# Keys and queries for pairs of tiles, a kept row made on ScalarE, and new orders, in a fused decoder layer

## The reference

```python
def _L0_attn_ref(...):                      # x = x + this(layernorm(x))
    t = tokens * rsqrt(mean(tokens * tokens) + eps) * rms_w
    gates = sigmoid(t @ w_gates)            # one per head
    q, k, v = t @ wq, t @ wk, t @ wv        # 8 heads of 64
    attn = softmax(where(causal_mask, -max, q @ k.T * scale))
    return sum over heads of ((attn @ v) * gates) @ wo

def _L0_xattn_ref(...):                     # x = x + this(layernorm(x), ctx, ctx)
    u = q @ k.T * scale / sqrt(8)           # 16 heads of 8, no projections
    logits = where(mask, -inf, tanh(u) * exp(log_C))
    return softmax(logits) @ v @ W_out.T

def _L0_ffn_ref(x, ...):                    # x = x + this(layernorm(x))
    xn = layernorm(x) * g + b
    probs = softmax(clip(xn @ router_w.T))
    topk_p, topk_i = top_k(probs, 2)        # 2 of 8 experts
    for eid in range(8):
        xe = xn * dense_gate[:, eid]
        hidden = silu(gate) * up            # of xe @ gate_up_w[eid].T
        out = out + hidden @ down_w[eid].T
    return x + out
```

## Time and profile before

| | us |
|---|---|
| median of 3 runs | 259.38 |
| lowest and highest run | 257.85, 260.14 |
| the profiled execution's own time | 259.18 |
| its span in the profile | 257.4 |
| busy in it: PE | 224.5 (87%) |
| busy in it: DVE | 197.1 (77%) |
| busy in it: ACT | 144.0 (56%) |
| busy in it: POOL | 128.2 (50%) |
| mean granted clock of PE | 0.958 of full speed |

### The profile page before, as it was taken

One profiled execution on the slowest core, in us unless ns is written; L12 is line 12 of the kernel. 1 busy time (PEld: TensorE's weight loads), 2 busy tenths in 40 slices (PEclk: granted clock), 3 DMA queues, 4 the chain that ended last, 5 costly groups with the idle time before them and its releaser, 6 DMA issues. The chain is left out here.

```text
span 257.4 us, 9580 instructions
## 1 busy us (share of the span) xinstructions
PE 224.5 (87%) x3360; PEld 184.5 (72%) x3360; DVE 197.1 (77%) x874; ACT 144.0 (56%) x333; POOL 128.2 (50%) x184
## 2 busy tenths in 40 slices
PE   8888999999999999999999988857987999989800
PEld 2666877886886887877777755436977899989700
DVE  2558687898898889989888897968995777766343
ACT  2455776885776776777667656424332355545400
POOL 1122321413546746646556356636777776656630
PEclk9999999999999999999999999975999999999965
DMA  7995999300000000000000001065774888888376
GB/s 221 254 374 215 401 410 406 135 3 4 3 12 26 14 13 24 14 13 25 13 14 21 16 0 35 24 174 179 218 216 116 268 275 230 268 239 250 94 237 190
DMA packets 24526, 36.31 MB, mean 141 GB/s; under 512 B 3726, under 2 KB 14225, under 8 KB 24224
## 3 DMA queue, kind: packets, MB, share of 16 engines
q1 hardware_dynamic: 20272, 29.98, 36.3%
q0 software_dynamic: 2272, 4.27, 4.7%
q10 hardware_dynamic: 1936, 1.46, 1.9%
HBM read 21.26 MB, written 14.89 MB: 140 GB/s over the span
## 5 line engine op out<-in xcount | busy, mean ns | idle before, releaser
L1959 POOL TENSOR_TENSOR rstd<-var,cst 128x1 f32<-128x1 f32 (+1 forms) x32 | 25.8, 807 | 73.8 <-DVE var L1300 48.7
L2058 POOL DMA_INDIRECT results<-y_sb,meta x39 | 38.3, 981 | 16.9 <-DVE xw_sb L1707 9.1
L505 PE MATMUL six<-gT_sb,gu_sb 128*128 128x128 f32 x312 | 43.3, 288 | 0.6 <-issue 0.6
L505 PEld LDWEIGHTS six<-gT_sb,gu_sb 128*128 128x128 f32 x312 | 39.4, 201 | 1.0 <-issue 0.8
L2016 POOL DMA_INDIRECT slots<-pay,slot_i x32 | 33.2, 1038 | 11.9 <-issue 7.0
L1093 ACT ACTIVATE jsilu<-six 128x256 f32<-128x256 f32 x39 | 14.9, 383 | 21.8 <-PE six L505 21.8
L1690 DVE TENSOR_TENSOR hidT<-jsilu,six 128x256 f32<-128x256 f32 x39 | 16.2, 416 | 10.7 <-PE six L505 10.7
L505 PE MATMUL six<-downT_sb,hidT 128*128 x156 | 23.6, 278 | 0.7 <-DVE hidT L1690 0.7
L1029 ACT ACTIVATE etanh<-six,xscale 128x1024 f32<-128x1024 f32 x16 | 17.8, 1113 | 7.1 <-PE six L505 7.1
L505 PEld LDWEIGHTS six<-downT_sb,hidT 128*128 128x128 f32 x156 | 20.3, 192 | 1.2 <-issue 1.1
L505 PEld LDWEIGHTS six<-wo_sb,oT_sb 128*128 128x128 f32 x128 | 15.5, 191 | 6.4 <-issue 6.4
(11 more groups left out here) (159 smaller groups left out, 537.8 us busy)
## 6 DMA issues: line engine op xcount, KB each, us to landing
gu_sb<-in_guT SPq DMA_DIRECT2D x39, 256.0 KB, 3.7
slots<-empty_sb SPq DMA_DIRECT2D x16, 528.0 KB, 5.9
g_sb<-slots SPq DMA_DIRECT2D x39, 66.0 KB, 3.4
ctxT_all<-in_ctxT SPq DMA_DIRECT2D x1, 1024.0 KB, 8.7
downT_sb<-in_downT SPq DMA_DIRECT2D x1, 1024.0 KB, 9.8
y_all<-results SPq DMA_DIRECT2D x4, 256.0 KB, 3.6
x_all<-in_x SPq DMA_DIRECT2D x2, 320.0 KB, 3.7
results<-y_sb,meta POOLq DMA_INDIRECT x39
```

What stands on the lines that cost most here:

```text
L505: return pe.matmul(o, lhsT=l, rhs=r, start=start, stop=stop, **kw)
L1959: nc.gpsimd.tensor_tensor(dst, src, half[:, 0:dst.shape[1]], ALU.pow).then_inc(semaphore, 1)
L2058: nc.gpsimd.indirect_dma_start(results, bass.IndirectOffsetOnAxis(meta[j % (2 * RING)][:, 0:1].bitcast(I32), 0), y_sb[k][:, :], None, boun ...
```

## The change

**Keys and queries.** `tT_sb` now holds two tiles side by side. `project_k` and `project_q` are replaced by `project_lo(n)` and `project_hi(n)`: with n even they make the keys of tiles n and n + 1, with n odd the queries of tiles n - 1 and n; lo makes the first four of the eight heads and hi the others, two products of 256 columns each. One n is done per step, two steps ahead of the tile, and `turn_t` and `normalize` run three ahead, so that the loop begins at i = -3. The number and the size of ACT's copies are as before.

**The kept row.** `norm_xhat` and POOL's `carry` go. POOL's `line` makes two numbers per row, 1 + rstd and -mean * rstd, and ACT's `carry` writes x2 * (1 + rstd) - mean * rstd in one Identity operation.

**Orders.** PE, DVE, ACT and POOL have new orders in `step` and in the drain.

```diff
-        tT_sb = several("tT_sb", [P, P])
-        qT_sb = several("qT_sb", [P, NJ, P])
-        k_sb = several("k_sb", [P, NJ, P])
+        tT_sb = several("tT_sb", [P, 2, P])
+        q_sb = several("q_sb", [P, NJ, 2, P], n=2)
+        k_sb = several("k_sb", [P, NJ, 2, P], n=2)
...
+            def project_pair(n, bank, j0):
+                w = wq_sb if n % 2 else wk_sb
+                both = tT_sb[n // 2 % BUFS].rearrange("p u t -> p (u t)")
+                for m in range(2):
+                    ins = mm(bank[:, m * 2 * P:(m + 1) * 2 * P], w[:, (j0 + m) * P:(j0 + m + 1) * P], both)
+                return ins
...
+            def project_lo(n):
+                after(pe, tT_ready, n | 1)
+                after(pe, lo_ready, n - 1)
+                after(pe, oT_ready, n - 3)
+                project_pair(n, ko_bank, 0).then_inc(lo_done, 1)
...
+            def project_hi(n):
+                after(pe, hi_ready, n - 1)
+                after(pe, pT_ready, n - 3)
+                after(pe, tanh_ready, n - 4)
+                project_pair(n, qp_bank, NJ // 2).then_inc(hi_done, 1)
...
             def scores(t):
-                after(pe, qT_ready, t)
-                after(pe, k_ready, t)
+                after(pe, lo_ready, query_fill(t))
+                after(pe, hi_ready, query_fill(t))
...
             def turn_p(t):
                 after(pe, weighed, t)
-                if has(t + 1, 0):
-                    after(pe, qT_ready, t + 1)
+                if has(t + 2, 0):
+                    after(pe, hi_ready, t + 2)
...
             def step(i):                                    (PE)
+                if has(i, 1):
+                    attend(i - 1)
                 if has(i, 0) and i > 0:
                     gates(i)
-                if has(i, 1):
-                    attend(i - 1)
-                if has(i, -1):
-                    turn_t(i + 1)
                 if has(i, 3):
                     cross_project(i - 3)
+                if has(i, -3) and i != -1:
+                    turn_t(i + 3)
...
-                    project_k(i + 1)
-                    project_q(i + 1)
+                if has(i, -2):
+                    project_lo(i + 2)
+                    project_hi(i + 2)
...
             def step(i):                                    (ACT)
                 if has(i, 4):
                     turn_xn(i - 4)
-                if has(i, 0):
-                    evacuate_q(i)
+                if has(i, -1):
+                    evacuate_lo(i + 1)
+                    evacuate_hi(i + 1)
                 if has(i, 1):
                     evacuate_v(i - 1)
+                if has(i, 4):
+                    carry(i - 4)
...
+            def carry(t):                                   (ACT)
+                after(act, line2_ready, t)
+                nc.scalar.activation(res_all[:, t], x2_sb[t % ROWS], ACT.Identity,
+                                     bias=line2[t % ROWS][:, 1:2],
+                                     scale=line2[t % ROWS][:, 0:1]).then_inc(res_ready, 1)
...
-            def norm_xhat(t):                               (DVE)
-                nc.vector.tensor_scalar(xhat[t % ROWS], x2_sb[t % ROWS], mv2[t % BUFS][:, 0:1], rstd2[t % BUFS][:, 0:1],
-                                        ALU.subtract, ALU.mult).then_inc(xhat_ready, 1)
...
-            def carry(t):                                   (POOL)
-                after(pool, xhat_ready, t)
-                nc.gpsimd.tensor_tensor(res_all[:, t], x2_sb[t % ROWS], xhat[t % ROWS],
-                                        ALU.add).then_inc(res_ready, 1)
+            def line(t):
+                after(pool, x2_rstd, t)
+                after(pool, res_ready, t - ROWS)
+                nc.gpsimd.tensor_scalar(line2[t % ROWS][:, 0:1], rstd2[t % BUFS][:, 0:1], 1.0, None, ALU.add)
+                nc.gpsimd.tensor_scalar(line2[t % ROWS][:, 1:2], mv2[t % BUFS][:, 0:1], rstd2[t % BUFS][:, 0:1],
+                                        -1.0, ALU.mult, ALU.mult).then_inc(line2_ready, 1)
...
-XSTEPS = (-1, 0, 2, 4, 6, 8, 10)
+XSTEPS = (-3, -2, 1, 3, 5, 7, 9)
```

More of the change, by code:

```diff
@@ L361, in tile_steps @@
         def tile_steps(step):
-            for i in range(-2, TAIL):
+            for i in range(-3, TAIL):
                 step(i)
@@ L615, in attend @@
                 after(pe, v_ready, t)
-                after(pe, k_ready, last(t + 1))
-                if not has(t + 1, 0):
+                after(pe, lo_ready, last(t + 2))
+                if not has(t + 2, 0):
                     after(pe, oT_ready, t - 1)
@@ L686, in turn_a @@
                 after(pe, a_ready, t)
-                after(pe, tT_ready, last(t + 3))
+                after(pe, tT_ready, last(t + 5))
                 after(pe, xnT_ready, t - 1)
@@ L710, in turn_xn @@
                 after(pe, xn_ready, t)
-                after(pe, tT_ready, last(t + 4))
-                if not has(t + 4, 0):
+                after(pe, tT_ready, last(t + 6))
+                if not has(t + 6, 0):
                     after(pe, egate_ready, last(t + 3))
@@ L794, in step @@
                     scores(i + 1)
+                if has(i, 2):
+                    turn_a(i - 2)
+                if i == -1:
+                    turn_t(2)
             tile_steps(step)
@@ L913, in _ @@
             route(14)
+            turn_g(0)
             cross_project(15)
-            turn_g(0)
             turn_g(1)
+            gate_up(0)
+            turn_xn(15)
             turn_g(2)
-            turn_xn(15)
+            route(15)
+            gate_up(1)
             turn_g(3)
-            route(15)
-            gate_up(0)
-            gate_up(1)
             gate_up(2)
-            down(0)
             turn_g(4)
@@ L988, in turn_t, with heads, evacuate_lo, evacuate_hi @@
                 after(act, t_turned, t)
-                nc.scalar.activation(tT_sb[t % BUFS], tr_ps, ACT.Copy,
+                nc.scalar.activation(tT(t), tr_ps, ACT.Copy,
                                      scale=vecs[:, 0:1]).then_inc(tT_ready, 1)
-            def evacuate_q(t):
-                after(act, q_done, t)
-                copy(qT_sb[t % BUFS], qk_ps).then_inc(qT_ready, 1)
-            def evacuate_k(t):
-                after(act, k_done, t)
-                copy(k_sb[t % BUFS], k_ps).then_inc(k_ready, 1)
+            def heads(n, j0):
+                pair = (q_sb if n % 2 else k_sb)[n // 2 % 2]
+                return pair[:, j0:j0 + NJ // 2].rearrange("p j u t -> p (j u t)")
+            def evacuate_lo(n):
+                after(act, lo_done, n)
+                copy(heads(n, 0), ko_bank).then_inc(lo_ready, 1)
+            def evacuate_hi(n):
+                after(act, hi_done, n)
+                copy(heads(n, NJ // 2), qp_bank).then_inc(hi_ready, 1)
             def gates(t):
@@ L1080, in step @@
                     turn_o(i - 1)
-                if has(i, -1):
-                    turn_t(i + 1)
+                if i == 0:
+                    turn_t(2)
+                if has(i, -3) and i != -1:
+                    turn_t(i + 3)
                 if has(i, 0):
@@ L1086, in step @@
                     cross_tanh(i - 2)
+                if i == 1:
+                    keep_norm()
+                if has(i, 2):
                     cross_exp(i - 2)
@@ L1495, in step @@
                     add_total(i - 7)
+                if has(i, 2):
+                    residual1(i - 2)
+                if has(i, 4):
+                    norm_x(i - 4)
+                if pair_at(i, 6):
+                    choose(i - 6, 11)
+                if has(i, 2):
+                    take_x1_stats(i - 2)
+                if pair_at(i, 6):
+                    choose(i - 6, 12)
                 if has(i, 1):
@@ L1514, in step @@
                 if pair_at(i, 6):
+                    choose(i - 6, 14)
+                if has(i, 1):
+                    invert(i - 1)
+                if has(i, 2):
+                    x1_variance(i - 2)
+                if pair_at(i, 6):
                     chosen(i - 6)
                     row_number(i - 6)
-                if has(i, 2):
-                    x1_variance(i - 2)
                 if has(i, 1):
                     weigh(i - 1)
+                if pair_at(i, 6):
+                    place_rows(i - 6, 0)
+                for n in range(2, len(XSTATS)):
+                    if i == XSTEPS[n]:
+                        x_statistics(*XSTATS[n])
                 if has(i, 2):
                     cross_query(i - 2)
+                if has(i, -3):
+                    normalize(i + 3)
+                if has(i, 4):
+                    clip_logits(i - 4)
                 if has(i, 3):
@@ L1869, in _ @@
             choose(14, 8)
+            weigh_rows(6)
             choose(14, 9)
-            gate(1)
             choose(14, 10)
```

404 lines of the change are left out of this document (177 added, 227 removed).

## The result

The changed kernel takes 265.67 us (median of 4 runs, 265.51 to 267.98), the kernel before 258.91 (4 runs). The ratio is 1.028, with a 95% interval of 1.021 to 1.036: **slower by 2.8%**; between the medians lie 6.8 us. The forecast was 259.6, the range ended at 264.5. Executions of one kernel differ by one or two per cent, and the slowest of them are put down to a slower state: ratios and spreads here are those of the others, medians are those of all runs. The profiled execution took 265.69 us, its span is 263.9.

What follows compares the result with a forecast made beforehand. PE was taken to set the loop step, with no engine full between 170 and 180 us. Start +1.9 net, products -0.8, order +0.9, drain -2.0 and +0.4 gave +0.4 on 259.18: 259.6 us, range 254 to 264.5.

Steps and rivals of the forecast that it cites:

- 0.3 later for `shift`, of which `oT`'s own delay covers half, five times: +0.7: DVE's ranking steps: two choosing operations between the maximum and shift delay cross_scores and project_o, +0.7 us.
- The slower rival: PE's cross_scores: waits from the new order around shift and oT cost 0.33 every step, 0.3 more in ranking steps; chance 0.25.
- The start: Before the loop: the first pair product waits for tile 1 and scores(0) for both matrices; +3.2 us.
- What comes back: Last loop step, without projection: tiles 2 and 3 done ahead return part of their 1.73 us, -1.3 us.
- The drain: After the loop: earlier gate_up(0) and fewer DVE operations before the second table; -2.0 us, between 0 and -4.4.
- `gate_up(0)`: PE's drain: behind the second turn_g it begins at about 173.7, not 176.69, moving 1.7 us of job work into idle time.
- The products: PE's keys and queries: eight 256-column records cost 1.73 us, 0.06 less per step, -0.8 us over 13 steps.
- The rival of wide products: PE's keys and queries: records cost their weight load, not columns; about 9 us less, 250.5; chance 0.05.
- The kept row: Loop steps: DVE's 0.34 us less per step counts nothing, as PE sets the step; ACT's copies hide behind PE.
- Route's wait: PE's router product: with V ahead of the ranking, its 0.27 us wait goes in five ranking steps, -1.4 us.

Runs made afterwards that it cites:

- e1: The changed kernel with choose(0) alone between row_max and shift, choose(1) to (4) behind shift, and shift(15) ahead of choose(10, 2) in the drain: 262.19 us, ratio 1.014.
- e6: e1 with the drain lists of the kernel before on PE, ACT, DVE and POOL: 262.99 us, ratio 1.015 to the kernel before.
- e9: The kernel before with the kept row and e1's step orders, but keys and queries per tile and the old drain: 260.57 us, ratio 1.006.
- e8: The changed kernel with choose(2) and choose(3) behind shift in the steps, choose(0) and choose(1) still ahead of row_max: 263.69 us in a single execution.
- e7: The kernel before with gate_up(0) moved behind the second turn_g, from behind the fourth and route(15): 258.73 us, ratio 1.000.
- e3: The changed kernel with warming products in the drain, 4 ahead of the first turn_g and 7 ahead of the second: 266.11 us, ratio 1.029.
- e5: e1 with DVE's second-table steps from gate(4) on, as in the kernel before, and PE's turn_table ahead of gate_up(8): 263.76 us, ratio 1.019.
- e4: The kernel before with the kept row alone made the new way, all other orders as before: 259.89 us, ratio 1.005.
- e10: The kernel before with PE making the values ahead of the ranking and of cross_attend: 265.03 us, ratio 1.022.

## Why the prediction was wrong, point by point

The sign was wrong, and the time lies 1.2 us above the range. Step by step from the changed kernel to the one before, the ratios fall by 1.4 points for the choosing operations (to e1), by nothing for the drain lists (to e6), by about 1.0 for the pairs (to e9; the intervals of e6 and e9 just overlap, the 3.5 us at `attend(1)` do not depend on them) and by 0.6 for what is left in e9, its join among it. That these add up to 2.8 is no evidence, since each step starts where the last ended.

- **The step that failed first: "0.3 later for `shift`, of which `oT`'s own delay covers half, five times: +0.7".** The place was right and the size wrong: the five ranking steps lose 3.0 us by it (after against e1). Two things were missed. The forecast counted only what stands between `row_max` and `shift`; `choose(0)` and `choose(1)` stand ahead of `row_max` and hold it up by some 0.5 us, 0.1 of it for ACT's exponential. And `choose(2)` and `choose(3)` take some 0.5 between `row_max` and `shift` and not 0.3: each took 0.3 to 0.4 us here, where the rows of before gave 0.17 for one. e1 and e8 show both.
- **The slower rival** had the right place, `cross_scores`. In the ranking steps its price of 0.33 + 0.3 us comes close to the 0.6 measured, but by luck, since 0.33 of it was for `oT`. That part was no loss: the copy starts 1.03 us after `attend` (0.76 before; 1.1 was forecast), and the plain step takes 9.13.
- **The start** was right in size: +3.2 forecast, +3.1 at full clock in five profiles, with the first scores at 12.5 to 12.6 (12.3 forecast), and +4.4 in the one after. What comes back was too high: 0.6 and not 1.3, and none of it in the step without projection, where PE waits instead.
- **The drain** failed as a mechanism: -2.0 forecast, of which `gate_up(0)` was 1.7 and gave nothing in e7. Job work moved into PE's idle time ahead of the table, but the end waits for PE only behind it, and there PE had as many products left as before. Ahead of the table no order on PE alone (e7) and no clock (e3) moved the copy by more than 0.4 us. Where DVE's list did move it, by 0.4 in e5 and 1.1 in e6, the span's end moved by 0.3 at most: that the table alone sets the end, as the forecast also had it, is not borne out either.
- **The products** were right: eight records of 256 columns take 88.96 to 90.69, 1.73 us as forecast. The rival of wide products falls, and with it, here, the rule of the Trainium skill ("TensorE: Matmul & The Clock Gate", section "Back-to-back issue gap") by which wider products would be cheaper per column: the traces do not agree with it for these float32 records, spaced 0.216 us at 256 columns and 0.111 at 128.
- **The kept row** was right: no gain and no measurable loss in the steps (e4).
- **Route's wait** went as forecast in the changed kernel, but e10 shows that the reason given, values ahead of the ranking, is not enough for it.

## What to carry to other kernels

In a hand-written order, an operation that is moved ahead of another is priced by all that then stands in the other's way: the operations in front of the whole chain and not only those between its two parts, at the distance at which they start there and not at the length of one, and with what the first of them waits for on other engines. Work moved into an engine's idle time gains only if the end waits for that engine there: count what is left for it behind the next point that another engine sets, and put a cheap experiment on it (warm it, or move the product alone) before it is counted. Work done ahead for two tiles at once cost its start in full here, and little of it came back, because the last step was not bound by the same engine.

## What the runs showed of the hardware

In the profile after, the first six distances between the keys' records were 0.40 to 0.46 us and the later ones 0.22, though the view of the stretch gives a granted clock of 1.00:

```profile
8.00:16.00 8.00, 6.57 (x59) 4.79 (x58) 2.62 (x11) 3.15 (x7) 1.09 (x1) 1.00 0.94 275
```
